# A gated feed-forward cut in chunks of 128 instead of 114 columns

## The reference

```python
h = shift_token(x)                     # the second half of the channels moves one token on
h = layernorm(h) * lg + lb
h = h @ w1 + b1                        # w1 is 256 x 1364
a, g = jnp.split(h, 2, axis=-1)        # value: columns 0:682, gate: columns 682:1364
h = a * jax.nn.gelu(g, approximate=False)
x = x + h @ w2 + b2                    # w2 is 682 x 256
```

## Time and profile before

| | |
|---|---|
| median of 3 runs | 1918.43 us (1913.34 to 1921.14) |
| the profiled execution | 1920.51 us, of which the span from the first to the last instruction is 1918.7 us |
| busy in the span | PE 1676.2, PE's weight loads 1285.8, DVE 1261.9, ACT 926.7, POOL 908.5 us |
| mean granted clock of TensorE | 0.941 of full |
| feed-forward of layer 0 | about 979 to 1204 us of the span |
| feed-forward of layer 1 | about 1686 to 1908 us |

### The profile page before, as it was taken

One profiled execution on the slowest core, in us unless ns is written; L12 is line 12 of the kernel. 1 busy time (PEld: TensorE's weight loads), 2 busy tenths in 40 slices (PEclk: granted clock), 3 DMA queues, 4 the chain that ended last, 5 costly groups with the idle time before them and its releaser, 6 DMA issues.

```text
span 1918.7 us, 37804 instructions
## 1 busy us (share of the span) xinstructions
PE 1676.2 (87%) x10522; PEld 1285.8 (67%) x10522; DVE 1261.9 (66%) x3658; ACT 926.7 (48%) x2530; POOL 908.5 (47%) x1070
## 2 busy tenths in 40 slices
PE   3778677999289999999969999399999999789997
PEld 1222366887168787787757778277787877678876
DVE  3666342766478778787645555388788887656765
ACT  1110112554268778788821222178778787711211
POOL 4100031666465555555435554465555555346665
PEclk8788787999699999999989999699999999989999
DMA  4100001021300000000010000200000000001011
GB/s 120 61 1 0 1 0 46 31 68 66 90 3 6 5 4 5 5 4 5 6 60 11 9 8 11 63 4 6 5 4 5 5 4 5 8 23 44 22 43 44
DMA packets 53430, 43.79 MB, mean 23 GB/s; under 512 B 9580, under 2 KB 51840, under 8 KB 53376
## 3 DMA queue, kind: packets, MB, share of 16 engines
q1 hardware_dynamic: 53376, 43.15, 7.2%
HBM read 26.37 MB, written 8.39 MB: 18 GB/s over the span
## 4 chain that ended last, share of the span: by engine, by line
PE 73%; DVE 6%; SPq 6%; DMA 5%; POOL 4%; issue 3%; ACT 2%; POOLq 1%; DVEq 0%; ACTq 0%; PEldq 0%; PEld 0%
PE bank L1446 7%; PE bank L1532 7%; PE bank L1500 6%; PE bank L1459 5%; PE bank L1374 5%; PE bank L1593 5%; PE bank L1594 5%; PE bank L1595 5%; PE bank L1376 5%; PE bank L1375 5%; SPq L465 4%; PE bank L1398 3%; PE bank L1214 3%; DMA x_in<-in_L_attn_hidden_states 2%; POOL h_lo L743 2%
## 5 line engine op out<-in xcount | busy, mean ns | idle before, releaser
L686 POOL TENSOR_TENSOR rnorm<-sumsq,neg_half 128x8 f32<-128x8 f32 x128 | 210.9, 1648 | 139.8 <-DVE sumsq L1941 139.8
L1008 ACT ACTIVATE prob<-prob,neg_max 128x256 f32<-128x256 f32 x512 | 260.9, 516 | 2.3 <-DVE neg_max L2022 2.2
L1127 ACT ACTIVATE gelu_sb<-bank,b_sb 114x512 f32<-114x512 f32 x96 | 66.2, 689 | 350.8 <-PE bank L1595 350.8
L700 POOL TENSOR_TENSOR qk_cos<-qk_cos,qk_sin 128x512 f32<-128x512 f32 x128 | 163.5, 1278 | 125.3 <-DVE qk_cos L1904 122.9
L784 POOL TENSOR_TENSOR act_lo<-act_full,act_hi 114x512 fp32r<-114x512 f32 x96 | 127.0, 1323 | 177.8 <-PE bank L1610 102.5
L1374 PE MATMUL bank<-wqkv_hi,hT_hi 128*128 128x512 f32 x384 | 177.6, 462 | 3.7 <-DVE hT_lo L1890 1.9
L1593 PE MATMUL bank<-h_hi,w_hi 128*114 128x512 f32 (+1 forms) x384 | 156.5, 407 | 20.9 <-POOL h_lo L743 11.0
L1376 PE MATMUL bank<-wqkv_hi,hT_lo 128*128 128x512 f32 x384 | 154.4, 402 | 0.0
L1375 PE MATMUL bank<-wqkv_lo,hT_hi 128*128 128x512 f32 x384 | 154.0, 401 | 0.0
L1594 PE MATMUL bank<-h_hi,w_lo 128*114 128x512 f32 (+1 forms) x384 | 153.5, 400 | 0.0
L2191 DVE SCALAR_TENSOR_TENSOR act_full<-bank,b_sb,gelu_sb 114x512 f32<-114x512 f32 x96 | 71.0, 739 | 125.4 <-PE bank L1595 125.4
(11 more groups left out here) (225 smaller groups left out, 4224.7 us busy)
## 6 DMA issues: line engine op xcount, KB each, us to landing
x_in<-in_L_attn_hidden_states SPq DMA_DIRECT2D x16, 512.0 KB, 3.4
x_scratch<-x_in SPq DMA_DIRECT2D x8, 512.0 KB, 4.2
f_x<-x_scratch SPq DMA_DIRECT2D x8, 512.0 KB, 4.1
out<-f_y SPq DMA_DIRECT2D x8, 512.0 KB, 3.0
hs_attn<-x_sb SPq DMA_DIRECT2D x16, 254.0 KB
hs_ffn<-x_sb SPq DMA_DIRECT2D x64, 63.5 KB
raw<-in_L_ffn_wqkv SPq DMA_DIRECT2D x2, 1536.0 KB, 6.7
raw<-in_L_ffn_w SPq DMA_DIRECT2D x2, 1364.0 KB
```

The costliest lines, as they stand in the source:

```text
L686: pool.tensor_tensor(rnorm[:, part * HEADS:(part + 1) * HEADS], sumsq[:, which * HEADS:(which + 1) * HEADS], neg_half[:, 0:HEADS], ALU.pow ...
L1008: act.activation(prob[:, h], prob[:, h], ACT.Exp, bias=neg_max[:, h:h + 1], scale=-1.0, accum_out=psums[:, h:h + 1]).then_inc(exped, 1)
```

## The change

The chunk width FW becomes 128. Five chunks make 640 columns (FULL), and 682 - 640 = 42 (REST) are left of gate and value each. For the last chunk both rests are placed side by side in the copy of w1: the gate's at columns 0 to 41 and the value's at columns 64 to 105 of one piece of 106 columns, with 22 unused columns between. So up(5) is one product of six matmuls in one bank, the gate in partitions 0 to 41 and the value in 64 to 105. DVE reads its value operand of chunk 5 from there and waits for g_ready alone. FC stays 6. w1 is loaded in four pieces (gate and value are no longer in the order of the tensor), and the tiles of w1 have W1C = 1386 columns. The gate's columns come first now.

```diff
-FW = 114
+FW = 128
+FULL = (FC - 1) * FW
+REST = HID - FULL
+REST_A = 64
+W1C = 2 * FULL + REST_A + REST
...
-        w1_hi = place("w1_hi", [P, DC, 2 * HID], F32R)
-        w1_lo = place("w1_lo", [P, DC, 2 * HID], F32R)
+        w1_hi = place("w1_hi", [P, DC, W1C], F32R)
+        w1_lo = place("w1_lo", [P, DC, W1C], F32R)
...
-                sp.dma_start(raw[:, 0:2, 0:2 * HID], w1[lay].rearrange("(c p) n -> p c n", p=P)).then_inc(raw_ffn, 16)
+                w1_in = w1[lay].rearrange("(c p) n -> p c n", p=P)
+                for to, first, n in ((0, 0, FULL), (FULL, HID, FULL), (2 * FULL, HID + FULL, REST), (2 * FULL + REST_A, FULL, REST)):
+                    sp.dma_start(raw[:, 0:2, to:to + n], w1_in[:, :, first:first + n]).then_inc(raw_ffn, 16)
...
-                pool.tensor_tensor(w1_lo[:, 1], raw[:, 1, 0:2 * HID], w1_hi[:, 1], ALU.subtract)
+                pool.tensor_tensor(w1_lo[:, 1], raw[:, 1, 0:W1C], w1_hi[:, 1], ALU.subtract)
...
-                    act.activation(w1_hi[:, c], raw[:, c, 0:2 * HID], ACT.Copy).then_inc(split_hi, 1)
+                    act.activation(w1_hi[:, c], raw[:, c, 0:W1C], ACT.Copy).then_inc(split_hi, 1)
...
-                    for to, first, done in ((0, HID, g_ps), (2, 0, a_ps)):
-                        if to == 2 and j >= 2:
+                    groups = ((bank[:, j % 2], FULL + j * FW, FW), (bank[:, 2 + j % 2], j * FW, FW))
+                    if j == FC - 1:
+                        groups = ((bank[0:REST_A + REST, j % 2], 2 * FULL, REST_A + REST),)
+                    for i, (to, first, n) in enumerate(groups):
+                        if i == 1 and j >= 2:
                             pe.wait_ge(act_ready, FC * k + j - 1)
-                        cols = slice(first + j * FW, first + j * FW + w)
+                        cols = slice(first, first + n)
                         for c in range(DC):
-                            pe.matmul(bank[0:w, to + j % 2], w1_hi[:, c, cols], h_hi[:, half, c], start=(c == 0), stop=False)
-                            pe.matmul(bank[0:w, to + j % 2], w1_lo[:, c, cols], h_hi[:, half, c], start=False, stop=False)
-                            mm = pe.matmul(bank[0:w, to + j % 2], w1_hi[:, c, cols], h_lo[:, half, c], start=False, stop=(c == DC - 1))
-                        mm.then_inc(done, 1)
+                            pe.matmul(to, w1_hi[:, c, cols], h_hi[:, half, c], start=(c == 0), stop=False)
+                            pe.matmul(to, w1_lo[:, c, cols], h_hi[:, half, c], start=False, stop=False)
+                            mm = pe.matmul(to, w1_hi[:, c, cols], h_lo[:, half, c], start=False, stop=(c == DC - 1))
+                        mm.then_inc((g_ps, a_ps)[i], 1)
...
-                        dve.wait_ge(a_ps, FC * k + j + 1)
+                        if j < FC - 1:
+                            dve.wait_ge(a_ps, (FC - 1) * k + j + 1)
+                            a = bank[0:w, 2 + j % 2]
+                        else:
+                            a = bank[REST_A:REST_A + REST, j % 2]
                         dve.wait_ge(g_ready, FC * k + j + 1)
...
-                        dve.scalar_tensor_tensor(out=act_full[0:w, j % 2], in0=bank[0:w, 2 + j % 2], scalar=b1_sb[0:w, 0, j:j + 1],
+                        dve.scalar_tensor_tensor(out=act_full[0:w, j % 2], in0=a, scalar=b1_sb[0:w, 0, j:j + 1],
                                                  in1=gelu_sb[0:w, j % 2], op0=ALU.add, op1=ALU.mult).then_inc(act_ready, 1)
```

More of the change, by code:

```diff
@@ L511, in _ @@
                 settle(sp)
-                sp.wait_ge(raw_ffn, 48 * (lay + 1))
+                sp.wait_ge(raw_ffn, 96 * (lay + 1))
                 settle(sp)
@@ L1099, in _ @@
                 act.activation(warm[:], warm[:], ACT.Gelu).then_inc(gate_exp, 1)
-                act.wait_ge(raw_ffn, 48 * (lay + 1))
+                act.wait_ge(raw_ffn, 96 * (lay + 1))
                 for c in range(DC):
-                    act.activation(w1_hi[:, c], raw[:, c, 0:2 * HID], ACT.Copy).then_inc(split_hi, 1)
+                    act.activation(w1_hi[:, c], raw[:, c, 0:W1C], ACT.Copy).then_inc(split_hi, 1)
                 raw_w2 = raw[:, 2, :].rearrange("p (c n) -> p c n", n=D)
@@ L2148, in _ @@
                 dve.wait_ge(split_hi, SPLITS * lay + DC + 1)
-                dve.tensor_tensor(w1_lo[:, 0], raw[:, 0, 0:2 * HID], w1_hi[:, 0], ALU.subtract)
+                dve.tensor_tensor(w1_lo[:, 0], raw[:, 0, 0:W1C], w1_hi[:, 0], ALU.subtract)
                 dve.wait_ge(hs_ffn_moved, 32 * (NB * lay + GB))
```

## The result

The kernel after took 1926.59 us in the median of 16 runs (1920.5 to 1934.69), the kernel before 1919.13 us beside it (16 runs, 1912.99 to 1922.93). The ratio is 1.0037, with a 95% interval of 1.0025 to 1.0049: slower by 0.37%, which lies within the 0.5% that I had called no change, but outside the range of 1907 to 1918. The profiled execution took 1924.64 us, its span is 1922.8.

What follows compares the result with a forecast made beforehand. The bound was the chain ending each group (up(5)'s value half, DVE, POOL act_lo and h_lo, PE), not PE's queue. 5.9 + 0.5 - 0.2 = 6.2 us saved gave 1912.2 us, 0.32% less; range 1907 to 1918.

Steps and rivals of the forecast that it cites:

- Partition counts: Chunks of 128 and 42 partitions in place of 114 and 112, in DVE, ACT, POOL and down: cost 0.
- rival D: PE's longer idle drops its clock to 1.2 GHz in each group: 42 us in 15 more groups, 1954 us; chance 0.02.
- The chain: Group end runs up(5)'s value half, DVE, POOL act_lo, h_lo, PE; 0.66 us gained in each of 9 groups, 5.9 us.
- B: No chain at the group's end; PE's saving counts in full, 22.3 us, giving 1896.1 us; chance 0.03.
- The lock: In seven layer-1 groups POOL's last_sum holds DVE's act_hi of chunk 5, which ends about 0.30 us behind it.
- A: act_hi of chunk 5 is not held by last_sum: 9.7 us saved, 1908.7 us; chance 0.12.
- The layer-1 term: Seven layer-1 groups where last_sum precedes act_lo(5): 0.07 us gained each, 0.5 us in all, bounds -0.4 and +4.0.
- Wider weights: Ten products per group with 128 stationary columns in place of 114: 0 taken, upper bound 2.4 us.
- odd partitions: act_full of chunk 5 reads partitions 64 to 105 and writes 0 to 41: 0 taken.
- C: Wider weight loads come onto PE's path inside the groups: 10.6 us cost, 1922.8 us; chance 0.07.
- E: Whole saving lost in places held for free, odd partitions above all: 1918 us; sign act_full over 0.75 us; chance 0.06.
- Loads and the split of w1: Ahead of the groups: w1's four-piece loads cost 0; extra columns in w_lo and w_hi copies cost 0.2 us in all.

Runs made afterwards that it cites:

- f1: Kernel after, but down(5) reads all 128 rows, with zero weights in w2 below its 42 rows; 1911.68 us, ratio 0.9946 to the kernel before.
- e3: Kernel before with chunk 5's value product (six matmuls per group) left out, chunks still 114 wide; 1913.76 us, ratio 0.9960 to the kernel before.
- e7: e1_fill with POOL's last_sum moved from ahead of act_lo(5) to behind norm_lo; 1906.78 us, ratio 0.9926 to the kernel before.
- e6: e1_fill with semaphore a_ps counted six per group, like g_ready; 1910.26 us, ratio 0.9940 to the kernel before.
- e2: Kernel before with chunk width 128 alone, up(5) still two products of 42 columns; 1914.88 us, ratio 0.9973 to the kernel before.
- g1: Kernel after with down(5) over 128 rows, a_ps counted six per group, half of norm_lo ahead of act_lo(5), last_sum last; 1891.84 us, ratio 0.9839.
- e1_fill: Kernel after plus six useless matmuls per group, three ahead of down(5) and three behind; 1910.8 us, ratio 0.9945 to the kernel before.

## Why the prediction was wrong, point by point

**The step that failed** is "*Partition counts* (128 and 42 in place of 114 and 112, in DVE, ACT, POOL and down) ... cost 0", and with it the 0.02 given to rival D. For the duration of the instructions it holds: down(5)'s first matmul with 42 rows lasts 0.38 us, with 112 it lasted 0.39, and DVE's act_full takes 0.75 us as before. What it left out is that matmuls of 42 rows behind PE's longer wait do not keep TensorE's clock at 2.4 GHz. The crossed pairs show it: with the long wait, 42 rows against 128 is 1.0037 against 0.9946, and 42 against 112 is 1.0109 against 0.9960. The clock's price in the change is the first difference, 0.91% or about 17 us; in the profiles it is (173.36 - 162.58) + (172.34 - 165.48) = 17.6 us, about 2 us for each of nine groups.

Rival D had the right place with the wrong reason against it. "A group that leaves PE without work for 1.34 us keeps 1.00, and 2.1 in two pieces is not much more": the 2.1 was near (2.01 in layer 0 and 2.27 in layer 1 of f1), and with 128 rows it does keep 1.00. I compared the idle time alone, where the change altered the rows at the same spot. D's price of 42 us was too high: not every group fell, and a fallen one lost 2.0 us on the mean, not 2.8.

**The chain** was right. 0.66 us per group of layer 0 was forecast; f1 shows 166.71 - 162.58 = 4.13 us in six groups, 0.69 each, and e3 shows 0.61 to 0.65 with nothing but the value half gone. B was wrong as argued: PE's full 1.395 us came in no kernel.

**The lock** was right in kind and size: act_hi ends 0.29 us behind last_sum, forecast 0.30, and A (act_hi not held) is excluded. The Trainium skill, "SBUF — State Buffer", section "Who interferes with whom", says that a DVE cast in a two-port mode and a GpSimd instruction exclude each other for the whole instruction; for last_sum and act_hi the trace now agrees, 1.20 us in place of 0.42. POOL's rstd over four elements held no act_hi. e7 shows what last_sum in that place costs, 0.55 us per layer-1 group, of which the lock's share is at most about 0.49.

**The layer-1 term** was mis-sized by 0.2 us per group: +0.14 (27.61 against 27.47) where -0.07 was forecast, 7 groups, +1.0 us for -0.5. Of that, 0.15 us is the register instruction between DVE's two waits (e6), which the sum did not have at all. What is left is some 0.06 us per group, inside the bounds that I gave for the released copy.

**Wider weights, odd partitions (C, E)**: nothing, as taken. e2's groups at a clock of 1.00 are no longer than those of the kernel before, and act_full from partition 64 takes 0.75 us. E's "places I hold for free" does cover the row counts, but its price (1918) and its sign (act_full over 0.75 us) did not come.

**Loads and the split of w1** were costed at 0 and 0.2 us lost. They gain: POOL's w_lo is 0.42 us shorter in each layer, and PE's wait ahead of layer 1 is 1.4 to 1.5 us shorter (24.63, in f1 24.70, for 26.12). w_lo takes 2.78 us in every kernel with 1386 columns and 3.20 in every one with 1364; why is open. "Cost 0" rested on the bytes being the same. For the wait, the shorter issues of b1's last piece are not reason enough: e2 has the same short issues, and PE waits 25.98 us there. What e2 lacks is the four-piece load of w1, which the kernels with 24.6 to 25.2 us all have; no run changes it alone, so the cause is not shown.

**Without the clock** the terms give 8 x 0.69 + 0.66 - 1.0 + 1.4 + 2 x 0.4 = 7.4 us for f1, and 9.5 were measured, with an interval of 7.3 to 13.4. The forecast's 6.2 was thus near for the kernel that it had in mind, in part by luck: the gains of 1.4 and 0.8 us ahead of the groups were not in it, and the layer-1 groups took 1.5 us back. In the two profiles some 1.5 us of what remains lie in layer 0's first group, 28.25 us in f1 against 30.43, of which the merged product explains 0.66: the clock of that group is 0.94 in f1 against 0.91. Why it starts so is open.

**Open** as well is where between 42 and 112 rows, and between 0.5 and 1.2 us of waiting, the clock begins to fall: only these values were run. Nor is it shown why some groups of the kernel after keep 1.00 with the same rows and waits as the fallen ones (that at 1768.98 in layer 1, with waits of 1.47 and 1.49 us), or why one group fell in e2 and in e3 each. So is whether g1's order would keep the clock with 42 rows. f1's rows from 42 on have zero weights, so it is rows in use by the instruction, and not work with a result, that kept the clock. Whether the rows count in the stationary or in the moving operand can't be told, since they are the same number.

## What to carry to other kernels

Where a change makes matmuls fewer or narrower, ask at the same spot how long PE then waits and how many rows the matmuls behind that wait use, read the granted clock of single groups, and pad the contraction to full rows with zero weights, which cost no matmul time here. Find first what ends a group: POOL's new order (half of norm_lo moved into a wait, last_sum last) was worth more (0.84%) than the removed matmuls with full rows (0.54%), and on top of it those were worth 13 us. Try to keep the counts of two semaphores that one instruction waits for the same, so that no register instruction stands between the waits; here it gave 0.15 us in a layer-1 group and no clear gain in the total.

## What the hardware showed that I had not expected

- TensorE's granted clock depended on the rows of a few matmuls. With 42 rows in place of 128 in twelve of a group's 147, and waits around them of up to 1.49 (1.47) and 0.80 us, 9 of 12 middle groups were slowed by falls to 1.2 GHz in place of 0. With 42 rows in place of 112 and waits of up to 1.35 and 0.81 us, it was 12 in place of 1.
- Six matmuls per group whose results nobody uses made the kernel 0.92% faster (e1_fill against the kernel after, both to before).
- A register instruction between two semaphore waits of a DVE instruction (act_full of chunk 4) moved its start from 0.20 to 0.36 us behind the start of the next product's first matmul.
- POOL's w_lo was faster over 1386 columns (2.78 us) than over 1364 (3.20), in every kernel and both layers.
